# Token rows behind the last up products, and the scan's first multiply ahead of token 0's work

## The reference

```python
h = _L0_tok_ref(x, ...)                      # 16-head attention
h = concat([cls_tok, h], axis=1)             # 513 tokens
h = h + _L0_attn_ref(_layernorm(h), ...)     # diagonal scan
h = h + _L0_ffn_ref(_layernorm(h), ...)      # quantised conv FFN
h = h + _L1_attn_ref(_layernorm(h), ...)     # selective scan, below
h = h + _L1_ffn_ref(_layernorm(h), ...)      # quantised gated FFN, below

# _L1_attn_ref, the recurrence of a selective scan with 16 states n:
dA = exp(dt_t[:, :, None] * A[None])
h  = dA * h + (dt_t * xv_t)[:, :, None] * B_t[:, None, :]
y_t = einsum('bdn,bn->bd', h, C_t)           # later y * silu(z), then @ W_out.T

# _L1_ffn_ref:
gate = silu(_bitlinear(x, w_gate))
up = _bitlinear(x, w_up)
return _bitlinear(gate * up, w_down)         # _bitlinear divides each token by its largest |value|,
                                             # rounds to 8 bits and multiplies the scale back
```

## Time and profile before

| | |
|---|---|
| median of 3 runs | 2511.28 us (2508.47 to 2514.41) |
| the profiled execution | 2506.92 us, span 2505.1 us, mean granted clock of PE 0.948 |
| PE busy | 2123.6 us (85%) |
| DVE busy | 2010.2 us (80%) |
| ACT busy | 1496.9 us (60%) |
| POOL busy | 1123.6 us (45%) |

### The profile page before, as it was taken

One profiled execution on the slowest core, in us unless ns is written; L12 is line 12 of the kernel. 1 busy time (PEld: TensorE's weight loads), 2 busy tenths in 40 slices (PEclk: granted clock), 3 DMA queues, 4 the chain that ended last, 5 costly groups with the idle time before them and its releaser, 6 DMA issues.

```text
span 2505.1 us, 26721 instructions
## 1 busy us (share of the span) xinstructions
PE 2123.6 (85%) x9288; PEld 1187.9 (47%) x9288; DVE 2010.2 (80%) x2418; ACT 1496.9 (60%) x2379; POOL 1123.6 (45%) x562
## 2 busy tenths in 40 slices
PE   4998879898798987989879888788978988878897
PEld 2236664345423765434532476543453256644345
DVE  7855889996885588998787467899878747799977
ACT  3654478774375447876637544787563744567844
POOL 2220249982221115997222111799622302279952
PEclk9999899998999988999999999899989999989997
DMA  6200000000210000000021000000003000000000
GB/s 213 83 1 1 18 0 1 1 1 1 90 56 1 1 17 0 1 1 1 2 101 43 1 1 17 1 0 1 1 11 108 27 1 1 1 1 1 1 0 18
DMA packets 41085, 51.43 MB, mean 21 GB/s; under 512 B 9072, under 2 KB 32368, under 8 KB 40944
## 3 DMA queue, kind: packets, MB, share of 16 engines
q1 hardware_dynamic: 40944, 49.62, 6.0%
HBM read 26.25 MB, written 10.49 MB: 15 GB/s over the span
## 4 chain that ended last, share of the span: by engine, by line
PE 39%; DVE 39%; ACT 9%; issue 8%; POOL 3%; DMA 1%; SPq 0%; DVEq 0%; ACTq 0%; POOLq 0%
DVE big L2071 17%; PE psum L806 12%; PE psum L950 5%; ACT big L1248 4%; PE psum L869 4%; PE psum L938 3%; ACT mid L1248 3%; PE psum L923 3%; PE psum L1105 2%; POOL big L2232 2%; PE psum L1137 2%; DVE negmax L1792 2%; DVE mid L1693 2%; PE psum L888 2%; PE psum L957 2%
## 5 line engine op out<-in xcount | busy, mean ns | idle before, releaser
L1248 ACT ACTIVATE big<-psum 128x512 f32<-128x512 f32 (+2 forms) x604 | 456.1, 775 | 275.1 <-PE psum L938 145.1
L2232 POOL TENSOR_TENSOR big<-big 128x2048 f32<-128x2048 f32 x124 | 561.9, 4531 | 40.3 <-DVE big L2071 40.0
L1105 PE MATMUL psum<-big,ident 128*128 128x512 f32 x992 | 505.3, 615 | 66.3 <-POOL big L2232 66.3
L2071 DVE TENSOR_TENSOR_SCAN big<-psum,b,big 128x512 f32<-128x512 f32 x404 | 490.0, 1263 | 6.9 <-ACT psum L1248 6.6
L1792 DVE TENSOR_REDUCE negmax<-psum 128x1 f32<-128x512 f32 x512 | 318.6, 678 | 43.8 <-PE psum L923 42.7
L1248 ACT ACTIVATE psum<-mid,aneg 128x512 f32<-128x512 f32 x404 | 268.5, 680 | 78.8 <-DVE big L2071 78.7
L1105 PEld LDWEIGHTS psum<-big,ident 128*128 128x128 f32 x992 | 173.8, 193 | 231.2 <-POOL big L2232 142.7
L923 PE MATMUL psum<-mid 96*128 96x512 bf16 x512 | 188.5, 388 | 32.8 <-DVE negmax L1792 12.2
L938 PE MATMUL psum<-mid 98*128 98x512 bf16 x512 | 182.3, 383 | 20.2 <-ACT big L1248 14.2
L1248 ACT ACTIVATE mid<-mid 128x513 f32<-128x513 f32 (+3 forms) x120 | 104.3, 883 | 154.7 <-DVE mid L2081 80.6
L2196 POOL TENSOR_TENSOR big<-big,mid 128x513 f32<-128x513 f32 x40 | 50.8, 1282 | 288.1 <-ACT big L1248 288.1
(11 more groups left out here) (230 smaller groups left out, 3810.8 us busy)
## 6 DMA issues: line engine op xcount, KB each, us to landing
mid<-big SPq DMA_DIRECT2D x192, 64.0 KB, 2.6
mid<-scratch SPq DMA_DIRECT2D x192, 64.0 KB, 2.2
scratch<-big SPq DMA_DIRECT2D x4, 1536.0 KB, 6.1
out<-hres SPq DMA_DIRECT2D x8, 513.0 KB, 3.8
onorm<-in_x SPq DMA_DIRECT2D x8, 512.0 KB, 4.4
big<-in_w SPq DMA_DIRECT2D x2, 1024.0 KB, 6.4
big<-in_wg SPq DMA_DIRECT2D x1, 1024.0 KB, 9.7
big<-in_wu SPq DMA_DIRECT2D x1, 1024.0 KB, 11.7
```

The source lines that it names most:

```text
L1105: mm = nc.tensor.matmul(y_psum[:, c], ident[:, :], st(1, k)[:, c], start=(n == 0), stop=(n == NS - 1))
L1248: return nc.scalar.activation(o, a, func, **kw)
L2071: V.tensor_tensor_scan(st(0, k)[:, c], decays(DT * k + c), bx, b0[:, p, n, c:c + 1], ALU.mult, ALU.add).then_inc(scanned, 1)
L2232: G.tensor_tensor(st(1, k), st(0, k), c_row(k).unsqueeze(1).broadcast_to([P, DT, S]), ALU.mult).then_inc(hc_ready, 1)
```

## The change

Two things are moved, and one semaphore is split.

1. PE makes the rows I3 and S3 of batch 0 behind U7 of batch 1, instead of ahead of U6. With the order of the products their slots change as well. ACT copies these rows one step later.
2. At the scan's start, `spread_b(0)` waits only for the Silu of the last z product that stood in its own slot (`LAST_Z` = 5) instead of all eight; the wait for all eight moves to `project_first`. DVE's `spread(0)` goes ahead of dx0, b0 and y0. POOL's dt*x of batch 1 no longer waits for b0; to allow it, the semaphore `dtx_ready` becomes one for each batch.

```diff
-BETWEEN = {4: (("T2", 1),), 8: (("I2", 1), ("S2", 1)), 16 + 12: (("T3", 0),), 16 + 14: (("I3", 0), ("S3", 0))}
+BETWEEN = {4: (("T2", 1),), 8: (("I2", 1), ("S2", 1)), 16 + 12: (("T3", 0),)}
...
+TAIL_FILLS += [("I3", 0), ("S3", 0)]
-AT_T2, AT_I2, AT_T3, AT_I3 = 2, 5, HT + 7, HT + 10
+AT_T2, AT_I2, AT_T3, AT_I3 = 2, 5, HT + 7, HT + 11
...
+LAST_Z = max(DT * p + int(n[1]) + 1 for (n, p), (s, _) in FILLS.items() if s == 3 and n[0] == "z")
...
-                pe.wait_ge(z_silu, DT * PAIR)
                 pe.wait_ge(bc_split, 6 * PAIR)
...
                 def spread_b(k):
                     if k:
                         pe.wait_ge(b_copied, k)
+                    else:
+                        pe.wait_ge(z_silu, LAST_Z)
...
                 def project_first():
+                    pe.wait_ge(z_silu, DT * PAIR)
                     pe.wait_ge(first_state, PAIR + 6)
...
+                token_rows(3, (0,))
                 def next_heads(c):
...
-                V.tensor_tensor(dx0[:, :, :], both[:, :, 2, :, 0], both[:, :, 0, :, 0], ALU.mult).then_inc(
...
+                spread(0)
+                dve.wait_ge(dt_ready, PAIR)
+                dve.wait_ge(m_silu, DT * PAIR)
+                V.tensor_tensor(dx0[:, :, :], both[:, :, 2, :, 0], both[:, :, 0, :, 0], ALU.mult).then_inc(
...
                 dve.wait_ge(first_state, PAIR + 6)
-                spread(0)
                 for k in range(PAIR * NS):
...
-                pool.wait_ge(first_state, PAIR + 4)
                 pool.wait_ge(dt_ready, PAIR)
                 pool.wait_ge(m_silu, DT * PAIR)
-                G.tensor_tensor(mid4(1, 3), mid4(1, 2), mid4(1, 0), ALU.mult).then_inc(dtx_ready, 1)
+                G.tensor_tensor(mid4(1, 3), mid4(1, 2), mid4(1, 0), ALU.mult).then_inc(dtx_ready[1], 1)
```

More of the change, by code:

```diff
@@ L535, in build @@
         dt_ready = signal("dt_ready")
-        dtx_ready = signal("dtx_ready")
+        dtx_ready = [signal(f"dtx_ready{p}") for p in range(PAIR)]
         b_spread = signal("b_spread")
@@ L1111, in turn_dtx @@
                     pe.wait_ge(c_copied, k + 1)
-                    pe.wait_ge(dtx_ready, p + 1)
+                    pe.wait_ge(dtx_ready[p], 1)
                     for q in range(QT):
@@ L1994, in turn_vectors @@
                 dve.wait_ge(m_silu, DT)
-                V.tensor_tensor(mid4(0, 3), mid4(0, 2), mid4(0, 0), ALU.mult).then_inc(dtx_ready, 1)
-                dve.wait_ge(dt_ready, PAIR)
-                dve.wait_ge(m_silu, DT * PAIR)
-                both = mid[:, :].rearrange("p (b n c t) -> p b n c t", b=PAIR, n=4, c=DT)
-                V.tensor_tensor(dx0[:, :, :], both[:, :, 2, :, 0], both[:, :, 0, :, 0], ALU.mult).then_inc(
-                    first_state, 1)
-                dve.wait_ge(first_state, PAIR + 2)
-                for p in range(PAIR):
-                    V.tensor_tensor(b0[:, p], dx0[:, p].unsqueeze(1).broadcast_to([P, NS, DT]),
-                                    first[:, p, 0:NS].unsqueeze(2).broadcast_to([P, NS, DT]), ALU.mult).then_inc(
-                                        first_state, 1)
+                V.tensor_tensor(mid4(0, 3), mid4(0, 2), mid4(0, 0), ALU.mult).then_inc(dtx_ready[0], 1)
                 def spread(k):
@@ L2013, in spread @@
                     m = b_dve(k)
-                    dve.wait_ge(dtx_ready, k // NS + 1)
+                    dve.wait_ge(dtx_ready[k // NS], 1)
                     V.tensor_tensor(st(0, k)[:, 0:m], mid4(k // NS, 3)[:, 0:m, 1:T],
@@ L2049, in finish_scan @@
                                         ALU.mult).then_inc(gated, 1)
+                spread(0)
+                dve.wait_ge(dt_ready, PAIR)
+                dve.wait_ge(m_silu, DT * PAIR)
+                both = mid[:, :].rearrange("p (b n c t) -> p b n c t", b=PAIR, n=4, c=DT)
+                V.tensor_tensor(dx0[:, :, :], both[:, :, 2, :, 0], both[:, :, 0, :, 0], ALU.mult).then_inc(
+                    first_state, 1)
+                dve.wait_ge(first_state, PAIR + 2)
+                for p in range(PAIR):
+                    V.tensor_tensor(b0[:, p], dx0[:, p].unsqueeze(1).broadcast_to([P, NS, DT]),
+                                    first[:, p, 0:NS].unsqueeze(2).broadcast_to([P, NS, DT]), ALU.mult).then_inc(
+                                        first_state, 1)
                 dve.wait_ge(z_silu, DT * PAIR)
@@ L2222, in spread_pool @@
                                     b_row(k).unsqueeze(1).broadcast_to([P, b_end(k) - m, S]), ALU.mult).then_inc(b_pool, 1)
-                pool.wait_ge(dtx_ready, PAIR)
+                pool.wait_ge(dtx_ready[0], 1)
                 spread_pool(0)
```

## The result

Five runs of the changed kernel gave 2493.78 to 2501.08 us, median **2497.86**; five runs of the kernel before beside them gave a median of 2508.72. The ratio is 0.995 with an interval of 0.9934 to 0.9966. I had predicted 2505 us with a range of 2499.5 to 2510.5: the sign was right, the gain of 10.9 us is 1.7 times the 6.5 of the sum, and the time lies outside the range.

What follows compares the result with a forecast made beforehand. Bound: DVE's chain through late maxima in the last block, and the y0, `spread(0)`, POOL chain at the scan's start. Terms 5.5 + 1.0 = 6.5 us off the median 2511.28 gave 2504.8, predicted as 2505 us, range 2499.5 to 2510.5.

Steps and rivals of the forecast that it cites:

- PE's line in part 1: Last block: U6 and U7 keep 1.72 us, next-turn products start at 624.3 as before, T3 of batch 1 0.9 earlier.
- the sum of 5.5 us: Part 1's gain in the last block: 1.3 us in each of three turns plus 1.6 in the last.
- rival D: PE stays at half clock in the next-turn products, four taking 7.5 us more: slower, 2521.4 us; chance 5%.
- The waits of part 1: Last block: sixth maximum waits about 3 us for ACT; first scaling 1.6 us earlier, second 1.3, meeting POOL's operation.
- the head start: Scan's start: DVE could scan 1.6 us earlier, but the gain shrinks to 0.25 a turn, 1.0 us in all.
- the half microsecond that I had named as a sign: Scan's start: POOL's first multiply by C stays within 0.5 us of its place, 11.1 us after the last z product.
- POOL gets through behind DVE's L1995: Scan's start: POOL's dt*x waits for DVE until 358.52 and ends at 363.03, half a microsecond earlier than before.
- Rival C: Scan's start: POOL holds up DVE's L1995, scan starts 1.4 us later, 5.6 in all: 2511.4 us; chance 8%.
- 0.15 later: Scan's start: y0 done at 363.9, 0.15 us later than before, as dx0 and b0 now lie on its path.
- A: Scan's start: the first multiply's head start survives, 1.6 us a turn, 6.5 instead of 1.0: 2499.3 us; chance 10%.
- B: Part 1 gives only PE's 0.9 in three turns, under 1 in the last; part 2 nothing: 2508.3 us; chance 25%.

Runs made afterwards that it cites:

- e1: Part 1 alone, the scan's start as in the kernel before: 2498.09 us, ratio 0.9965 to the kernel before.
- e12: The kernel before plus the unused PE products of e10, the nine standing ahead of I3 and S3 of batch 0: 2490.64 us, ratio 0.9937.
- e10: Part 1 alone plus unused PE products at the scan's start, ahead of U6 and in the down projection's gap: 2487.14 us, ratio 0.9916.
- e4: The changed kernel with ACT's copies of I3 and S3 behind all absolute values of U6 and U7: 2497.77 us, ratio 0.9965.
- e5: The changed kernel with the 16 small products of `project_first` made twice: 2511.89 us, ratio 1.0004.
- e7: The changed kernel plus 9 unused products in PE's wait ahead of U6: 2501.76 us, ratio 0.9966.
- e11: e9 plus 9 unused PE products ahead of G4 of batch 0 and 8 ahead of T3 of batch 1: 2475.48 us, ratio 0.9867.
- e9: The changed kernel plus unused PE products at the scan's start, ahead of U6 and between the down projections (not last turn): 2487.28 us, ratio 0.99.
- e13: e11 without part 2, the scan's start as in the kernel before: 2487.63 us, ratio 0.9919.

## Why the prediction was wrong, point by point

**The step that failed is PE's line in part 1, and with it the sum of 5.5 us; 8.7 were measured from u to the turn's end (8.15 in e1).** The step reads: "PE's next-turn products start at 624.3 as before, and T3 of batch 1 at 628.8 - 0.86 = 627.9". It rested on this: "It was at half clock, 0.50, in these rows, so U6 and U7 keep the 1.72 us that they took with most of it at that level". PE's level is not a property of the place. Before, a wait of 2.58 us stood ahead of the rows, and rows, U6 and U7 all ran at 0.50. With the up products in front the level was back within the rows (e1, turn 0: 3.41 us) or never fell there (changed kernel, turn 0: 2.75). So PE began the next-turn products 3.6 us after u in turn 0 (5.0 in e1), not 6.5; T3 then waited for DVE alone, and batch 1's rows began 1.5 us earlier after u (1.7 in e1), not 0.9. Only turn 2 of the changed kernel had 0.2, with a dip behind T3. The second scaling therefore began 1.5 to 1.7 us earlier in every turn instead of 1.3 in three of them: 6.3 in all (6.9 in e1).

The other 2.4 us (1.2 in e1) lie between the second scaling and the turn's end, for which the sum had no term. There PE's level stood higher in the down projection. The last turn shows that part by itself, in the timelines of before and after:

```profile
2489.05 9.92 PE L888 MATMUL psum<-mid,wd 128*128 128x257 bf16 x64 [0.74 <-ACT mid L1248]
```

```profile
2484.49 8.65 PE L891 MATMUL psum<-mid,wd 128*128 128x257 bf16 x64 [0.74 <-ACT mid L1256]
```

That is 1.27 us; with the 1.5 by which the second scaling came earlier it makes the 2.8 that this turn gained (33.09 to 30.29). It can go the other way too: in turn 1 the second scaling came 1.75 earlier and the turn's end only 0.9. With full clock in rows and up products the order is worth 2.4 to 3.1 (e12 against e10), so some 5 us or more of e1's 8.15 hang on PE's half clock, as far as two kernels with added products can tell. In part 1 the prediction had the clock only as rival D, the side on which it is lost.

**The waits of part 1** were right in kind. The first scaling came 1.52 us earlier (1.6 predicted), the second 1.52 (1.3), in turn 0. The order was not, and that the first number came out is in part luck: in turn 0 of the changed kernel the fast rows let ACT copy early, POOL started at 622.37, and the *fifth* maximum lost the port. The chain gives it 3.63 us, to 0.6 after POOL's end at 625.45. The Trainium skill ("SBUF — State Buffer", section "Who interferes with whom") has this exclusion, and 5.99 us for four maxima, 5.71 for a scaling and 3.62 for another bear it out. So engines meet not only at semaphores, as I wrote of the chip: DVE and POOL meet at this port as well. The price of the collision was nearly the same wherever it fell, which is why e4 gained nothing. The second scaling kept its 2.82 us in turn 0, since POOL's second operation ended 0.34 us ahead of it, not after it.

**Part 2** was sized about right by luck, for a wrong reason. I expected the small products to slow down by at most 0.45 us and the head start to shrink to 0.25 a turn, 1.0 in all. In fact they sped up in two turns of four (1.92 us), and the first multiply gained 1.4 to 1.5 there, more than the half microsecond that I had named as a sign; in turn 3 they took 3.54, and it came 0.2 later than before. What reached the scan's end was lost again at the rows I2 and S2 of batch 1, a place that the prediction doesn't mention. Net: nothing beside part 1, 3 us alone.

**POOL and DVE at the scan's start.** Predicted: POOL gets through behind DVE's L1995. Measured: POOL's L2221 shows 5.86 us from 359.16; DVE ended at 360.64, and 4.51 behind that is 365.15, against the measured 365.02. Rival C, POOL first, did not happen. y0 took 0.35 us, as predicted (0.4), and was done 2.7 us after z, before 2.8; I had 0.15 later.

**Rivals.** A came closest in number (2499.3) and is refuted in mechanism (e5). B is refuted: part 1 gave more than PE's 0.9 a turn in three turns of four (2.8, 0.9, 2.2 and 2.8). D as a whole is refuted: the next-turn products took 1.98 and 1.88 us in turn 0. A small piece of it came in turn 2, where the first of those behind T3 took 2.99 us at a granted clock of 0.63, and the second scaling 3.53.

**The base.** The sum started from 2511.28, the median of three runs. With two runs more it was 2508.72 beside the result, 2.6 lower; the later series of the same kernel gave 2507.04 (17 runs), 2510.54 (20), 2507.77 and 2508.44 (9 each). Some 1 to 4 us of the miss of 7.1 are this.

## What to carry over

An edit that reorders PE's work also decides in which of its instructions a dip of the clock falls. Before summing durations, mark which rows of the trace were at the lower level, what wait stood ahead of them, and price each at both levels. A gain of 1.4 us a turn can vanish three stages later because the dip has moved onto narrow f32 products that others wait for. Unused products in PE's waits brought more here (2498 to 2475 us, ratio 0.9964 to 0.9867) than the reordering itself (2508 to 2498), but not in every wait: ahead of U6 alone (e7) they brought nothing, since the dip came back in front of the next rows. And when a collision of DVE and POOL on the port is moved, ask where it lands: it cost the same at the fifth maximum, the sixth, and the scaling.

## What the runs showed that I had not expected

The best kernel, e11, is 32 us (1.3%) below the kernel before, though each turn holds up to 75 products more whose result nobody reads, some 18 us of PE's time (nine take 2.12); its mean granted clock is 0.971 against 0.948.

The same wait can leave different levels behind it. In e9 and e10 PE waited 2.48 us ahead of G4 in both, and the rows behind took 4.08 us in one and 2.75 in the other. What decides it was not tried. The traces show this much: without part 2, the rows I2 and S2 of batch 1 took 2.75 us in each turn in which the small products at the scan's start had stayed at 1.95 (turn 1 of before, turns 1 and 2 of e1, every turn of e10, e12 and e13), and 4.0 in the others. With part 2 they took 3.5 to 4.3 in every turn of every kernel but e11, also behind small products of 1.92 us.

`spread(0)`, with one input in PSUM, took 1.75 us beside POOL's L2221 as it did alone, while instructions with both inputs in SBUF were held up for whole operations of POOL.
